# Five single-pass products of rounded parts for the experts' second product, on 128 rows

## The reference, cut to what matters

```python
xn = _layernorm(x, axis=-1)
x = x + _L1_attn_ref(xn, ...) + _L1_ffn_ref(xn, ...)

# in _L1_attn_ref: the dense inner rows
u, g = jnp.split(y @ w_swiglu.T, 2, axis=-1)          # 1024 inner rows
return x + u * jax.nn.silu(g) @ w_out.T

# in _L1_ffn_ref: H = 256, I = 176, E = 16, K = 2
topk_w, topk_idx = jax.lax.top_k(scores, K)
gu = jnp.einsum('th,ehj->etj', x, w_gate_up)           # first product
h = _swiglu(gu, I)                                     # silu(g) * u, 176 wide
y = jnp.einsum('eti,eih,te->th', h, w_down, combine)   # second product
y = y + _swiglu(x @ shared_gate_up, SI) @ shared_down  # dense, 352 inner rows
```

## Time and profile before

| | us |
|---|---|
| median of 3 runs | 506.21 (506.1, 506.21, 516.81) |
| profiled execution, span | 506.1 |
| TensorE busy in it | 489.5 (97%) |
| VectorE, ScalarE, GpSimd busy | 342.6, 297.2, 275.6 |
| first `xup`, last `xdown` start | 331.6, 479.0 |

### The profile page before, as it was taken

The page is one execution under the profiler, slowest core; times in us unless marked ns, Lnnn a source line. Parts: engine busy times, 40 slices in busy tenths (PEclk is TensorE's granted clock), DMA queues, the critical chain, the costliest instruction groups (busy, mean ns, idle before and its releaser), DMA issues.

```text
span 506.1 us, 7336 instructions
## 1 busy us (share of the span) xinstructions
PE 489.5 (97%) x2418; PEld 374.1 (74%) x2418; DVE 342.6 (68%) x732; ACT 297.2 (59%) x590; POOL 275.6 (54%) x253
## 2 busy tenths in 40 slices
PE   7999999989999999999999999999998999999997
PEld 5455557767887678879888888877766767677785
DVE  6999999898989999558989996224232322322347
ACT  5897898978899678589456343354331342323220
POOL 0163758749474566473634466847765665555500
PEclk9999999899999999999999999999999999999999
DMA  8900003004532011044105675722244222222177
GB/s 305 331 2 0 0 2 124 2 0 159 175 126 87 2 42 43 1 133 155 59 2 180 204 233 184 253 84 77 84 135 144 75 82 76 73 73 80 67 283 236
DMA packets 20245, 55.35 MB, mean 109 GB/s; under 512 B 3361, under 2 KB 6097, under 8 KB 20209
## 3 DMA queue, kind: packets, MB, share of 16 engines
q1 hardware_dynamic: 15696, 42.56, 24.7%
q0 software_dynamic: 4512, 12.33, 7.8%
HBM read 37.18 MB, written 17.74 MB: 109 GB/s over the span
## 4 chain that ended last, share of the span: by engine, by line
PE 71%; ACT 7%; POOL 6%; DMA 5%; issue 5%; DVE 4%; another core or an unknown queue 1%; SPq 0%; DVEq 0%; ACTq 0%
PE bank L317 50%; PE bank L510 9%; DMA y_rows<-m_y,dest 5%; PE bank L411 3%; POOL y_rows L1508 2%; POOL xg L1496 2%; PE bank L499 1%; PE bank L543 1%; PE bank L384 1%; ACT L643 1%; PE bank L570 1%; DVE m_y L1356 1%; PE bank L458 1%; ACT fd L729 1%; PE bank L400 1%
## 5 line engine op out<-in xcount | busy, mean ns | idle before, releaser
L1508 POOL DMA_INDIRECT y_rows<-m_y,dest x47 | 47.5, 1010 | 38.9 <-DVE m_y L1356 30.4
L1356 DVE TENSOR_SCALAR m_y<-bank,gslot 128x256 f32<-128x256 f32 x47 | 22.3, 483 | 61.1 <-DMA y_rows<-m_y,dest 36.6
L317 PE MATMUL bank<-mw,m_xt 128*128 x188 | 61.5, 463 | 0.8 <-DVE hs L1233 0.6
L1496 POOL DMA_INDIRECT xg<-xn_rows,tab x47 | 45.6, 971 | 20.2 <-issue 10.5
L317 PE MATMUL bank<-yhr,wsg_h 128*128 128x512 f32 x128 | 52.8, 412 | 0.0
L317 PE MATMUL bank<-hyr,wsg_h 128*128 128x512 f32 x128 | 50.0, 391 | 0.0
L317 PE MATMUL bank<-yhr,wsg_l 128*128 128x512 f32 x128 | 49.9, 390 | 0.0
L317 PE MATMUL bank<-mw,m_ht 88*128 x188 | 46.2, 381 | 3.1 <-DVE m_y L1356 2.0
L317 PEld LDWEIGHTS bank<-mw,m_xt 128*128 128x128 f32 x188 | 33.6, 189 | 17.8 <-issue 4.5
L1437 POOL TENSOR_TENSOR tk<-tk 128x512 f32<-128x512 f32 x16 | 21.0, 1315 | 38.0 <-ACT tk L787 37.9
L317 PEld LDWEIGHTS bank<-mw,m_ht 88*128 88x128 f32 x188 | 33.8, 190 | 8.7 <-issue 4.0
(11 more groups left out here) (272 smaller groups left out, 1393.5 us busy)
## 6 DMA issues: line engine op xcount, KB each, us to landing
mw<-in_gu SPq DMA_DIRECT2D x16, 352.0 KB
ga<-y_rows SPq DMA_DIRECT2D x8, 512.0 KB, 6.7
mw<-in_dn SPq DMA_DIRECT2D x16, 176.0 KB
wsg_w<-in_wsg SPq DMA_DIRECT2D x4, 512.0 KB, 4.2
spilled_x<-fa SPq DMA_DIRECT2D x4, 512.0 KB, 2.8
hx<-spilled_x SPq DMA_DIRECT2D x4, 512.0 KB, 4.6
xn_rows<-fg SPq DMA_DIRECT2D x4, 512.0 KB, 4.1
spilled_y<-fa SPq DMA_DIRECT2D x4, 512.0 KB, 3.0
```

Source lines behind the costliest of these rows:

```text
L317: mm = e.matmul(o, a, b, start=n == 0, stop=n == len(terms) - 1)
L1356: e.tensor_scalar(m_y[j % 3][:, :], ps("jd", j)[:, 0:D], gslot[:, j:j + 1], None, ALU.mult).then_inc(s["jy"], 1)
L1496: e.indirect_dma_start(out=xg[j % GATHERED][:, :], out_offset=None, in_=xn_d, in_offset=bass.IndirectOffsetOnAxis(ap=tab[:, j:j + 1], axis ...
L1508: e.indirect_dma_start(out=y_d, out_offset=bass.IndirectOffsetOnAxis(ap=dest[:, j:j + 1], axis=0), in_=m_y[j % 3][:, :], in_offset=None).t ...
```

## The change

1. **`xdown`** becomes five fp32r products of 256 columns on 128 rows. The hidden tile is now 256 wide: columns 0 to 127 are inner rows 0 to 127, columns 128 to 175 are inner rows 128 to 175, and columns 192 to 239 hold those last 48 again; the rest is zero (`jpad`, once). `hturn` transposes two full halves of 128. The weights of the last 48 rows lie as a high part on partitions 0 to 47 and as a low part on 64 to 111 of one tile `wb`, so that one product of it takes both.
2. **New work per expert**: `mround(n)` on ScalarE (one copy of 128 x 512 to the rounded high part) and `mlow(n)` on VectorE (a subtraction of 128 x 256 and one of 48 x 256). `dn` arrives on 128 partitions, 256 KB, in a raw area of four (later two) places, so loads now wait for `mlow`; the expert takes EW = 1472 words.
3. **New work per tile** on VectorE: `jhlow` (128 x 256) and a second, 48 wide multiplication in `jtimes`. `jsilu` writes to a buffer of its own.
4. **`SPLIT[2]`** False: the 11 `dlow` of batch 2 go from GpSimd to VectorE.
5. **The small input `vec`** is folded into `cst`: one load less at the start.
6. **All the orders are written anew.** `experts(0)` stands behind `rspill(3)`, `experts(7)` waits also for `table` on VectorE (semaphore rt at 22), three chunks of batch 3 instead of two go ahead of or among the first tiles, `breathe` stands in two blocks, 0 to 12 ahead of the gathers (waiting for rt at 22), 13 to 22 at the end.

```diff
-SPLIT = (True, True, True, False)
+SPLIT = (True, True, False, False)
-EW = 2 * 352 + 2 * D
+UW, DW = 2 * 352, 3 * D
+EW = UW + DW
@@ xdown
-                q.wait_ge(s["jtc"], j + 1)
+                if j == 0:
+                    q.wait_ge(*low_of(E - 1))
+                q.wait_ge(s["x1"], 2 * NB + j + 1)
                 r = place[j]
-                products(o[:, 0:D], [(m_ht[j % 3][:, c * P:(c + 1) * P], mw[0:88, bass.DynSlice(r + (704 + c * D), D)]) for c in range(2)]).then_inc(s["jd"], 1)
+                w, wl, wb = (mw_r[:, bass.DynSlice(r + (UW + k * D), D)] for k in range(3))
+                h, l = m_ht[j % 3]
+                terms = [(h[:, 0:P], w), (h[:, 0:P], wl), (l[:, 0:P], w), (h[:, P:2 * P], wb), (l[:, P:2 * P], wb)]
+                products(o[:, 0:D], terms).then_inc(s["jd"], 1)
@@ scalar
+            def mround(n):
+                q.wait_ge(d_mw[n % 2], 16 * STAGED.count(n % 2) + 32 * (n // 2 + 1))
+                o = n * EW + UW
+                hi = mw_r[:, o:o + 4 * D].rearrange("p (z n) -> p z n", n=2 * D)[:, :, 0:D]
+                e.activation(hi, raws[n], ACT.Copy).then_inc(s["ph"], 1)
@@ vector
+            def jhlow(j):
+                q.wait_ge(s["jtc"], j + 1)
+                h, l = m_ht[j % 3]
+                e.tensor_tensor(l[:, :], ps("jt", j)[:, 0:D], h[:, :].bitcast(F32), ALU.subtract).then_inc(s["x1"], 1)
+
+            def mlow(n):
+                q.wait_ge(s["ph"], len(PREP) + n + 1)
+                o = n * EW + UW
+                raw = raws[n]
+                b = mw_r[64:112, o + 2 * D:o + 3 * D]
+                e.tensor_tensor(mw_r[:, o + D:o + 2 * D], raw[:, 0, :], mw_r[:, o:o + D].bitcast(F32), ALU.subtract)
+                e.tensor_tensor(b, raw[64:112, 1, :], b.bitcast(F32), ALU.subtract).then_inc(low_of(n)[0], 1)
@@ sync, experts(n)
+                if n == EARLIER:
+                    q.wait_ge(*low_of(n - 1))
+                    q.wait_ge(s["rt"], 22)
+                elif n > EARLIER + 1:
+                    q.wait_ge(*low_of(n - 2))
+                elif 3 < n < EARLIER:
+                    q.wait_ge(*low_of(n - 4))
```

More of the change, by code:

```diff
@@ L142, in build @@
         at[0] = top_at
[L143 to L146, removed]
+        at[0] = E * EW
+        assert at[0] >= top_at
+        at[0] += 2 * D
+        xg = [tile(f"xg{n}", D) for n in range(3)]
         assert at[0] <= top_at + 3072
@@ L608, in tensor @@
[L608 to L611, removed]
@@ L616, in tensor @@
-            hturn(10, 2); xdown(6, 1); xdown(7, 5); xdown(8, 3); dgate(3, 2, 4); xup(12, 2); xup(13, 1); hturn(11, 3); xturn(15, 2); xturn(16, 5)
-            xup(14, 0); xup(15, 2); xdown(9, 1); xdown(10, 4); hturn(12, 3); hturn(13, 0); dup(3, 2, 5); hturn(14, 2); hturn(15, 0); xdown(11, 4)
-            xturn(17, 1); xturn(18, 5); xdown(12, 3); xdown(13, 4); ddown(3, 1, 6, 7); xdown(14, 3); xturn(19, 0); xturn(20, 5); xup(16, 1)
-            xup(17, 2); xup(18, 0); dgate(3, 3, 4); dgate(3, 4, 1); dup(3, 3, 3); xdown(15, 0); hturn(16, 2); xup(19, 5); xturn(21, 2); xturn(22, 0)
@@ L628, in tensor @@
-            xdown(33, 0); xup(39, 3); xup(40, 1); xdown(34, 5); xdown(35, 2); xdown(36, 0); xturn(42, 5); xturn(43, 4); xup(41, 2); hturn(37, 4)
-            hturn(38, 5); dgate(3, 5, 3); xup(42, 2); xup(43, 1); hturn(39, 5); xturn(44, 0); xdown(37, 4); xdown(38, 5); hturn(40, 2); hturn(41, 0)
-            xdown(39, 4); ddown(3, 4, 6, 7); xturn(45, 0); xturn(46, 5); xdown(40, 4); xdown(41, 2); hturn(42, 3); xup(44, 4); xup(45, 1)
-            xup(46, 5); hturn(43, 4); hturn(44, 1); hturn(45, 0); xdown(42, 3); xdown(43, 5); xdown(44, 1); hturn(46, 3); dup(3, 5, 0); xdown(45, 3)
@@ new lines, in tensor @@
+            xup(14, 0); xup(15, 5); xturn(17, 1); hturn(12, 3); xup(16, 4); xdown(10, 1); xdown(11, 3); xdown(12, 2); hturn(13, 0); hturn(14, 5); hturn(15, 1)
+            xup(17, 3); xturn(18, 2); xturn(19, 0); xturn(20, 4); xturn(21, 5); dgate(3, 3, 1); dgate(3, 4, 2); hturn(16, 0); xup(18, 3); xdown(13, 1)
+            xdown(14, 2); xdown(15, 4); hturn(17, 3); xup(19, 5); xup(20, 1); hturn(18, 2); xup(21, 4); xdown(16, 0); xdown(17, 3); hturn(19, 5); dup(3, 3, 2)
+            dup(3, 4, 1); hturn(20, 4); hturn(21, 0); xturn(22, 5); xdown(18, 3); xdown(19, 2); xdown(20, 1); xdown(21, 4); xturn(23, 5); xturn(24, 0)
@@ L634, in tensor @@
+            xturn(46, 0); hturn(44, 5); xdown(42, 3); hturn(45, 1); xdown(43, 2); xup(46, 0); xdown(44, 4); xdown(45, 5); hturn(46, 3); ddown(3, 4, 6, 7)
+            xdown(46, 2); dup(3, 5, 1); dup(3, 6, 0); dup(3, 7, 4); dup(3, 8, 3); dgate(3, 5, 5); dgate(3, 6, 2); dgate(3, 7, 5); dgate(3, 8, 1); dgate(3, 9, 2)
+            ddown(3, 5, 6, 7); ddown(3, 6, 6, 7); ddown(3, 7, 6, 7); dgate(3, 10, 0); dup(3, 9, 5); dup(3, 10, 4); ddown(3, 8, 6, 7); ddown(3, 9, 6, 7)
             ddown(3, 10, 6, 7)
@@ L1413, in gpsimd @@
+            jout(43); jhlow(45); jtimes(46); jout(44); jhlow(46); jout(45); jout(46); dtimes(3, 5); dtimes(3, 6); dlow(3, 5); combine(0, 0); combine(0, 1)
+            dlow(3, 6); dtimes(3, 7); combine(1, 0); combine(1, 1); combine(2, 0); dtimes(3, 8); dtimes(3, 9); combine(2, 1); combine(3, 0); dtimes(3, 10)
+            combine(3, 1); dout(3, 0); dout(3, 1)
         @block.gpsimd
```

438 lines of the change are left out of this document (242 added, 196 removed).

## The result

| | kernel before | changed kernel |
|---|---|---|
| median of the runs | 506.7 us | 522.8 us (520.4 to 525.0) |
| ratio | 1 | 1.029 (95%: 1.024 to 1.034) |
| span of the profiled execution | 506.1 us | 519.1 us |
| first `xup` / last `xdown` | 331.6 / 479.0 us | 345.8 / 489.1 us |

The forecast was 501.0 us (491 to 512). The result is slower by more than 2%, outside the range. The experiments add what one comparison can't show: the same changed kernel takes 496 us on one chip and 522 us on two others, while the kernel before takes 506 to 509 on all of them.

A forecast was written before the change was run, and what follows sets the result against it. TensorE was taken to bound the kernel, busy 489.5 of 506.1 us. The sum was 506.1 - 12.6 (`xdown`) + 1.2 (GpSimd among the tiles) + 7.1 (expert loads) - 0.8 (start) = 501.0 us, range 491 to 512.

The forecast's parts named there:

- The length of the tiles' stage: From first `xup` to last `xdown`: about 120 us, with TensorE's other waits left as they are, give or take 3.
- wrong altogether: Sign against the whole forecast: TensorE idles more than 25 us in sum, or in places the prediction doesn't name.
- xdown: Second product of the experts: five products at 0.119 us, 0.596 a tile instead of 0.865, saving TensorE 12.6 us.
- Rival 5: Register-addressed `xdown` products keep 0.216 us each: 10.1 us more instead of 12.6 less, 523.7 us; chance 0.04.
- The new order: All engines' lists: the rest of the new order only moves the same products, so no term of its own.
- The loads: Expert loads 7 to 15: `table` at 314, rounds of 6.4 us, last landing 4.7, end at 344.3; TensorE stands 7.1 us.
- Where the stall lies: TensorE waits 4 to 10 us just ahead of the first `mw,m_xt` product, near 337 to 345 us.
- GpSimd among the tiles: GpSimd's queue at 2.56 us a tile is level with TensorE; adds 1.2 us; `jout` waits fall from 30 to under 20.
- rival 2: GpSimd paces the tiles, needing 106 us for 83 DMAs plus `jout` waits; stage ends about 6 later, 507; chance 0.15.
- New work per tile: VectorE's `jhlow` and 48 wide multiplication: 0.73 us a tile, 34 us in all, hidden by TensorE's 2.2 us a tile.
- The start: ScalarE's first work no longer waits for `w_vec` until 5.73: 0.8 us earlier, bounds 0 and 1.2.
- a long chain of loads: Rival: the chain of expert loads is at its long end, 18 us instead of 7.1, giving 511.9; chance 0.08.

The follow-up runs named there:

- d0_after: The changed kernel unaltered, run on chip 10, against the kernel before: 496.2 us, 0.981.
- d1_orderalone: The kernel before with only the changed kernel's five lists, silu going to a buffer of its own, on chip 10: 499.1 us, 0.986.
- c0_after: The changed kernel unaltered, run on chip 5, against the kernel before: 521.5 us, 1.026.
- a1_spread: The changed kernel with a breathe pair after every fourth indirect DMA, on chip 15: 496.6 us against 505.6 of the kernel before, 0.979.
- e3_newdmas: The kernel before with GpSimd's gathers and scatters in the changed kernel's order, breathe pairs where they were, on chip 4: 516.7 us.
- e0_after: The changed kernel unaltered, run on chip 4, against the kernel before: 521.9 us, 1.027.
- f1_twounderway: The changed kernel with GpSimd starting an indirect DMA only when the one before the last has landed, on chip 4: 519.6 us.
- e2_olddmas: The kernel before with the changed kernel's lists, but GpSimd's gathers, scatters and breathe pairs in their old order, on chip 4: 538.2 us.
- b1_lump: The kernel before with breathe pairs 0 to 12 ahead of the first gathers and 13 to 22 behind the last scatter: 512.2 us, 1.012.

## Why the prediction was right or wrong

**The length of the tiles' stage** is the step that failed. I gave it about 120 us and let TensorE's other waits stand, give or take 3. d0_after shows the stage that I forecast: the first `xup` at 344.35 (344.3 forecast, and that it fits so closely is luck: load 15 went out at 337.57, 2.0 sooner than forecast, and `xup(0)` came 6.8 us after it instead of 4.7) and the last `xdown` 119.8 us later.

```profile
345.00:465.00 120.00, 119.53 (x692) 94.99 (x691) 64.63 (x204) 46.12 (x145) 83.15 (x86) 1.00 0.34 106
```

TensorE is busy 119.5 of 120 us. In the first comparison the same stage takes 143.3 us. Of the 24.9 us between the two spans (519.1 and 494.2) 23.5 lie here, 1.4 ahead of it and none behind. 18.0 of them are idle time of TensorE (32.8 against 14.8) and 6.9 are longer products (busy 486.3 against 479.4): the granted clock of the stage, 1.00 in d0_after, is 0.97. I looked for what could be late in TensorE, the loads and GpSimd's queue, and had no term for engines standing while their inputs are ready, although the trace of before showed one such wait of 2.9 us. I had written that I am wrong altogether if TensorE idles more than 25 us in sum; it idled 32.8. What the runs showed in place of the step is these waits; what releases them stays open.

**xdown.** Right: 0.12 us apart, 0.60 a tile. Rival 5 is false. But the saving comes to the span only in part: d0_after is 2.9 us below d1_orderalone, where the terms that part them (12.6 less 1.2 and 7.1) give 4.3, and the earlier start 0.3 more. By the traces the stage is 9.2 us shorter (129.0 to 119.8) and starts 5.7 later.

**The new order**, which I took as "only moves the same products", was the largest mis-sized term on such a chip: 499.1 against 506.4 us, 7.2 gained by the lists alone (TensorE's idle time falls from 16.6 to 11.5 us). I had put it at nothing without a reason. On the other sort of chip the same lists lose: 514.4 against 508.6.

**The loads.** Right in most terms: `table` at 313.74 (314), `mlow` 0.42 + 0.49 (0.85), rounds of 5.96, 5.87, 6.71 and 6.37 us (6.4), the first `xup` at 345.80 (344.3). The sum hides misses of either sign: the rounds end 0.7 us sooner than forecast, and the last landing, from load 15 at 338.88 to its `mround` at 344.66, took 5.8 us instead of 4.7, with 1.1 more until `xup(0)`. The landings of loads 7, 9, 11 and 13, up to the start of their `mround`, took 4.4, 4.3, 5.2 and 4.8 us. The Trainium skill ("DMA: Bandwidth & Descriptors", section "Why a DMA increments its semaphore by 16 and not by 1") leads to 4.1; the traces don't decide it, since the landings differ by 0.8 us from round to round, and by 2.7 before.

Where the stall lies was wrong. Of 5.8 us without work between 310 us and `xup(0)` only 1.2 stand ahead of `xup(0)`, not 4 to 10. I had looked at what queues behind the last `mround` and `mlow` and not at what queues behind the first: `dround(2, 6)` and `dlow(2, 6)` stand in their lists behind `mround(7)` and `mlow(7)`, and these wait for load 7. So `ddown(2, 6)` is late:

```profile
318.38 0.63 ACT L928 ACTIVATE mw_r<-raw 128x512 fp32r<-128x512 f32 x1 [6.23 <-DMA raw<-in_dn]
318.92 0.61 ACT L913 ACTIVATE hq0r<-hs 128x512 fp32r<-128x512 f32 x1
```
```profile
319.05 0.42 DVE L1410 TENSOR_TENSOR mw_r<-raw,mw_r 128x256 fp32r<-128x256 f32 x1 [2.25 <-ACT mw_r L928]
...
319.94 0.69 DVE L1278 TENSOR_TENSOR hs0r<-hs,hq0r 128x512 fp32r<-128x512 f32 x1
```
```profile
320.69 0.38 PE L537 MATMUL bank<-wout_h,hq0r 128*128 128x256 f32 x1 [2.52 <-DVE hs0r L1278]
...
322.27 0.42 PE L537 MATMUL bank<-wout_h,hq1r 128*128 128x256 f32 x1
322.48 0.42 PE L537 MATMUL bank<-wout_l,hq1r 128*128 128x256 f32 x1
```

After that idle time TensorE's products go at 0.12 us for 1.4 us and then at 0.21 (granted clock 0.52 from 322 to 325, the lower of its two levels, 1.2 GHz); the products until 325.63 cost 1.5 us more that I had no term for.

**GpSimd among the tiles.** On a chip without the waits it is as forecast (waits for `jout` 13.2 us, under 20), and rival 2 is false. **New work per tile** on VectorE is hidden: TensorE is busy 119.5 of 120 us (the 1.55 us a tile of the prediction should be 1.59: 40.4 and 34.3 over 47). **The start**: ScalarE begins at 5.41 instead of 5.73, 0.3 us and not 0.8, since it now waits for the larger `w_cst`.

**The rivals.** I had a slower result only as a slow product or a long chain of loads. The cost was in neither.

## What stays open

What releases the standing engines, and what makes one chip, or one moment, differ from another: five groups on four chips (one of them twice) gave two of the one sort and three of the other, and which chip the first comparison ran on isn't recorded. Slower indirect DMAs are not it: from 345 to 480 us they have landed 2.4 us after their start (median) in c0_after and in d0_after alike. Instruction transfers weren't tested as a cause. Those that the traces list (two queues) don't explain the longest wait of c0_after (none between 415.1 and 436.2 us), others fall into a wait (at 436.2 and 441.5 us), and whether these are all isn't known; the Trainium skill ("Runtime: NRT & Kernel Launch", section "Instruction fetch mechanics") calls their cost mostly hidden, and no run here shows otherwise. That the waits go with at most two DMAs under way, and when they end, ties them to the indirect DMAs; how is argued, not shown.

## What to carry to other kernels

A kernel can be 2% faster on one chip and 3% slower on another, steadily on each, and an edit measured on a single chip then seems to cure what only the chip had changed: run the unaltered kernel beside every edit, on the same chip. In lists that run in order, look at what stands behind every wait that an edit adds, the first as well as the last. Read a wait for an unnamed releaser, even a single one of 3 us, as a term with a range, and look whether indirect DMAs follow each other without a pause around it.

## What the runs showed of the hardware

- The same program takes 496.2 us (chip 10) and 521.5 to 522.0 (chips 5 and 4); on chip 15 (a1_spread) its form with the pairs spread takes 496.6. The kernel before takes 505.6 to 508.6 on all four.
- On chips 4 and 5 ScalarE, VectorE and GpSimd have waits for an unnamed releaser of 0.3 to 7.1 us (7.1 in e3_newdmas), up to 40.5 us in sum (e0_after), among gathers and scatters 1.28 us apart. Of the one of 6.3 us before `jhcopy(23)` in c0_after the input stood ready for 4.6. With at most two under way (f1_twounderway): none; in e2_olddmas none either, without that limit.
- An indirect DMA of 128 rows of 1 KB has landed 2.4 us after its start (median from 345 to 480 us), on chip 5 (c0_after) as on chip 10 (d0_after).
- In the first comparison and in d0_after TensorE, after 2.5 and 2.4 us without work, went on at full clock for 1.4 and 0.7 us and then at half clock for some 3.4 us (0.21 us between products of 256 columns, 0.12 otherwise).
- A pair of 48 wide memsets on GpSimd costs 0.27 us of its queue (b1_lump).
